# First attention: position tables in two sets of 64 rows, added in the tile shape of the paired scores, over their nonzero columns

## The reference, cut to what matters

```python
# DIM = 128, HEADS = 8, DIM_QK = 64, MAX_POS = 10; x is [4, 1024, 128]
x = x + attention(layernorm(x))
def attention(x):
    q, k, v = projections(x)                      # 8 heads of 64 (q, k) and 16 (v)
    dots = einsum('bhid,bhjd->bhij', q, k) * 64 ** -0.5
    dist = clip(seq[None, :] - seq[:, None], -10, 10) + 10
    attn = softmax(dots + conv[:, dist])          # conv is [8, 21]
    return (attn @ v) @ W_out + b_out
x = x + graph_of_six_attention_nodes(layernorm(x))
```

## Time and profile before

| | before |
|---|---|
| median of 3 runs | 3493.89 us (3486.42 to 3496.42) |
| the profiled execution's own time | 3510.56 us |
| its span | 3508.8 us |
| PE busy | 3152.7 us (90%), 18239 matmuls |
| DVE busy | 2418.2 us (69%) |
| ACT busy | 2154.6 us (61%) |
| mean granted TensorE clock | 0.922 of 2.4 GHz |

### The profile page before, as it was taken

How to read it: one execution, slowest core, us unless ns; L and a number is a source line. 1 busy time by engine, 2 the same in 40 slices (tenths; PEclk the granted TensorE clock), 3 DMA queues, 4 the chain that set the end, 5 groups by cost and what they waited for, 6 DMA issues and landing times. The chain is left out here.

```text
span 3508.8 us, 47634 instructions
## 1 busy us (share of the span) xinstructions
PE 3152.7 (90%) x18239; PEld 1353.8 (39%) x18239; DVE 2418.2 (69%) x3087; ACT 2154.6 (61%) x2695; POOL 389.8 (11%) x330
## 2 busy tenths in 40 slices
PE   5799999999748999999999999999999999999994
PEld 4355555555423333333333333333333333333331
DVE  5545544545146678888788788888778888787753
ACT  1144544544513467777777777777777777777683
POOL 0000000000010011111101111111111111111013
PEclk9699999999955589999999999999999999999897
DMA  5000000000043244344343344434444344443302
GB/s 160 16 10 4 22 1 10 16 10 10 17 119 73 46 94 100 89 96 91 77 95 90 79 100 102 100 90 96 75 92 94 91 94 85 102 100 86 60 22 80
DMA packets 144026, 244.99 MB, mean 70 GB/s; under 512 B 56290, under 2 KB 92534, under 8 KB 140726
## 3 DMA queue, kind: packets, MB, share of 16 engines
q1 hardware_dynamic: 143222, 239.85, 30.4%
q10 hardware_dynamic: 576, 2.10, 0.1%
HBM read 165.00 MB, written 74.10 MB: 68 GB/s over the span
## 5 line engine op out<-in xcount | busy, mean ns | idle before, releaser
L1395 ACT ACTIVATE pt_b<-ps_max 128x1024 f32<-128x1024 f32 x1516 | 1496.0, 1024 | 528.1 <-PE ps_max L1246 523.5
L1428 DVE TENSOR_REDUCE mx_b<-ps_pair 128x2 f32<-128x1024 f32 (+1 forms) x1032 | 1244.8, 1206 | 262.3 <-PE ps_pair L1232 255.4
L1282 PE MATMUL ps_ctx<-pt_b,vs 128*32 128x512 f32 x6144 | 866.6, 638 | 3.8 <-ACT c_b L1384 3.5
L1428 DVE TENSOR_REDUCE mx_b<-ps_misc 128x1 f32<-128x512 f32 x1032 | 706.2, 684 | 191.5 <-PE ps_misc L1232 174.7
L1246 PE MATMUL ps_max<-qs,ks 50*128 50x512 f32 x3032 | 828.6, 453 | 3.7 <-DMA qs<-mpart 3.1
L1232 PE MATMUL ps_pair<-ks,qs 48*128 48x512 f32 x2040 | 571.6, 487 | 128.2 <-DVE mx_b L1428 99.4
L1232 PE MATMUL ps_misc<-ks,qs 48*128 48x512 f32 x1032 | 491.8, 477 | 54.3 <-DVE mx_b L1428 47.8
L1246 PEld LDWEIGHTS ps_max<-qs,ks 50*128 50x128 f32 x3032 | 383.4, 196 | 354.5 <-ACT pt_b L1395 231.4
L1232 PEld LDWEIGHTS ps_pair<-ks,qs 48*128 48x128 f32 x2040 | 236.2, 197 | 462.2 <-DVE mx_b L1428 391.1
L740 ACT ACTIVATE pt<-ps_max,cb 128x512 f32<-128x512 f32 x342 | 215.6, 684 | 292.1 <-PE ps_max L617 227.6
L1232 PEld LDWEIGHTS ps_misc<-ks,qs 48*128 48x128 f32 x1032 | 204.5, 198 | 413.7 <-DVE mx_b L1428 332.7
(11 more groups left out here) (178 smaller groups left out, 2421.3 us busy)
## 6 DMA issues: line engine op xcount, KB each, us to landing
partd<-part SPq DMA_DIRECT2D x24, 2048.0 KB, 9.1
qs<-partd SPq DMA_DIRECT2D x288, 128.0 KB, 5.6
ks<-partd SPq DMA_DIRECT2D x288, 128.0 KB, 6.7
xq<-node SPq DMA_DIRECT2D x24, 512.0 KB, 3.9
xk<-node SPq DMA_DIRECT2D x24, 512.0 KB, 4.9
xv<-node SPq DMA_DIRECT2D x24, 512.0 KB, 5.8
xf<-node SPq DMA_DIRECT2D x24, 512.0 KB, 4.7
node<-nt_b SPq DMA_DIRECT2D x48, 256.0 KB, 2.2
```

What stands on the lines that cost most here:

```text
L1282: ins = pe.matmul(psO[SLOT * i:SLOT * i + SLOT, :], vs[u % 2][:, kb, QUAD * (s // HALF_STEPS) + i], pt[:, (QUAD * S + i) % ENTRIES], start ...
L1395: act.activation(pt[:, e:e + 2].rearrange("p k n -> p (k n)"), at[:], ACT.Exp, scale=SCALE_B).then_inc(exp_done, 1)
L1428: nc.vector.tensor_reduce(mx2[:, at:at + n], (psP, psX)[p % 2][:, 0:CHUNK * n].rearrange("p (h n) -> p h n", h=n), AX.X, ALU.max).then_inc ...
```

## The change

The table matrix is cut into two sets of 64 rows (keys 0 to 63 and 64 to 127 of the block: b = 0 and 1), kept per head in the partitions of that head: even heads of a pair in partitions 0 to 63, odd heads in 64 to 127. Each set enters as a pair of 64-row matmuls, one for each head, in the same tile shape as the pairs of L612 and L588. The weights are `eye`: for set b the identity of 64 in columns 64 b to 64 b + 63 of a 64 x 128 matrix, zero elsewhere. `side_half` cuts the columns by which a set is zero. The widths become 74 and 138 columns (r = 0 and 3), 202 and 266 (r = 1 and 2), and 10 for one set alone (r = 4 and -1). A score round with a table so has 8 table matmuls in four pairs (10 columns: 4 in two pairs) where it had 4; a maxima round 4 in two pairs (10 columns: 2 in one) where it had 2. Each half gains 96 matmuls and 96 weight loads.

The prelude loads the tables by 16 DMAs where it had 4, each 64 partitions by 4 heads, and turns them with `flip`, two exchange matrices of 64 on the diagonal, which DVE builds (one memset and two copies) before its first layernorm. At the start of the first attention DVE clears `eye` and fills it with four copies, where it made one copy of the identity.

```diff
+def side_half(kb, qc, b):
+    s, lo, hi, at = side(kb, qc)
+    if hi and s == 0 and b == 0:
+        hi = max(0, hi - DQK)
+    if hi and s == 1 and b == 1:
+        lo, at = lo + DQK, at + DQK
+    return s, lo, hi, at
...
-                    sp.dma_start(tabf[:, k], bass.AP(ext.tensor, k * HEADS * NE + first, [[1, P], [NE, HEADS], [1, WIN]])
-                                 ).then_inc(tab_in, D16)
+                    for odd in range(2):
+                        for b in range(2):
+                            src = bass.AP(ext.tensor, (k * HEADS + odd) * NE + first + DQK * (1 - b),
+                                          [[1, DQK], [2 * NE, HEADS // 2], [1, WIN]])
+                            sp.dma_start(tabf[DQK * odd:DQK * odd + DQK, k, b], src).then_inc(tab_in, D16)
...
+                dve.wait_ge(id_in, 2 * D16)
+                nc.vector.memset(flip[:], 0.0).then_inc(flipped, 1)
+                dve.wait_ge(flipped, 1)
+                for k in range(2):
+                    rows = slice(DQK * k, DQK * k + DQK)
+                    ins = nc.vector.tensor_copy(flip[rows, rows], exch[rows, DQK * (1 - k):DQK * (2 - k)])
+                ins.then_inc(flipped, 1)
...
+                def windows_of(kb, qc):
+                    found = [(b, *side_half(kb, qc, b)) for b in range(2)]
+                    return [w for w in found if w[3] > w[2]]
...
# maxima
-                    for odd in range(2 if hi else 0):
-                        ins = pe.matmul(to[:, CHUNK * odd + lo:CHUNK * odd + hi], idr[:],
-                                        tabM[:, s, QUAD * q + 2 * j + odd, at:at + hi - lo], start=False, stop=True)
+                    for half_, s, lo, hi, at in windows:
+                        for odd in range(2):
+                            rows = slice(DQK * odd, DQK * odd + DQK)
+                            ins = pe.matmul(to[:, CHUNK * odd + lo:CHUNK * odd + hi], eye[rows, half_],
+                                            tabM[rows, s, half_, 2 * q + j, at:at + hi - lo], start=False,
+                                            stop=half_ == windows[-1][0])
...
# score
-                    for odd in range(2 if hi else 0):
+                    for half_, side_, lo, hi, at in windows:
                         for k in range(2):
-                            ins = pe.matmul(to[:, CHUNK * odd + lo:CHUNK * odd + hi], idr[:],
-                                            tabS[:, k, side_, QUAD * q + 2 * j + odd, at:at + hi - lo], start=False,
-                                            stop=k == 1)
+                            for odd in range(2):
+                                rows = slice(DQK * odd, DQK * odd + DQK)
+                                ins = pe.matmul(to[:, CHUNK * odd + lo:CHUNK * odd + hi], eye[rows, half_],
+                                                tabS[rows, k, side_, half_, 2 * q + j, at:at + hi - lo], start=False,
+                                                stop=k == 1 and half_ == windows[-1][0])
...
-                nc.vector.tensor_copy(idr[:], sid[:])
+                nc.vector.memset(eye[:].bitcast(F32), 0.0).then_inc(eye_cleared, 1)
+                dve.wait_ge(eye_cleared, 1)
+                for b in range(2):
+                    for odd in range(2):
+                        rows, cols = slice(DQK * odd, DQK * odd + DQK), slice(DQK * b, DQK * b + DQK)
+                        nc.vector.tensor_copy(eye[rows, b, cols], sid[rows, rows])
```

More of the change, by code:

```diff
@@ L128, in program @@
         stored = ctx.enter_context(nc.semaphore("node_stored"))
-        with nc.sbuf_tensor("tab_scores", [P, 2, 2, HEADS, WIN], F32R) as tabS, \
-                nc.sbuf_tensor("tab_maxima", [P, 2, HEADS, WIN], F32R) as tabM:
+        with nc.sbuf_tensor("tab_scores", [P, 2, 2, 2, HEADS // 2, WIN], F32R) as tabS, \
+                nc.sbuf_tensor("tab_maxima", [P, 2, 2, HEADS // 2, WIN], F32R) as tabM:
             prelude(nc, psM, psS, psX, sid, exchange, x_rows, conv, conv_rev, ew, act_w, We, be, Wq, Wk, Wv, Wo, ident,
@@ L178, in prelude @@
         wfs = sb("wfs", [P, NODES, WF_COLS])
-        tabf = sb("tabf", [P, 4, HEADS, WIN])
+        tabf = sb("tabf", [P, 4, 2, HEADS // 2, WIN])
         exch = sb("exch", [P, P])
+        flip = sb("flip", [P, P])
         x_in = [sem(f"x_in{b}") for b in range(BATCH)]
@@ L194, in prelude, with table @@
             sem("wb_copied"), sem("wo_ready"))
-        def table(n):
-            return tabS[:, 0, n // HEADS, n % HEADS] if n < 2 * HEADS else tabM[:, n // HEADS - 2, n % HEADS]
+        flipped = sem("flipped")
+        def table(n, k=0):
+            t, b, pair = n // HEADS, n % HEADS // QUAD, n % QUAD
+            return tabS[:, k, t, b, pair] if t < 2 else tabM[:, t - 2, b, pair]
         with nc.Block() as block:
@@ L275, in _ @@
                     pe.matmul(psX[:, 36:37], wnin[:, c, 3], bcol[:, 0:1], start=True, stop=True).then_inc(wb_ready, 1)
-                pe.wait_ge(tab_in, 4 * D16)
+                pe.wait_ge(tab_in, 16 * D16)
+                pe.wait_ge(flipped, 2)
                 for n in range(4 * HEADS):
@@ L280, in _ @@
                         pe.wait_ge(tab_copied[n % 2], n // 2)
-                    pe.matmul(psS[n % 2][:, 0:WIN], exch[:], tabf[:, n // HEADS, n % HEADS], start=True,
+                    pe.matmul(psS[n % 2][:, 0:WIN], flip[:], tabf[:, n // HEADS, n % HEADS // QUAD, n % QUAD], start=True,
                               stop=True).then_inc(tab_ready, 1)
@@ L385, in _ @@
                             dve.wait_ge(tab_high[0], n // 2 + 1)
-                        nc.vector.tensor_tensor(tabS[:, 1, (n + k) // HEADS, (n + k) % HEADS], psS[k][:, 0:WIN],
+                        nc.vector.tensor_tensor(table(n + k, 1), psS[k][:, 0:WIN],
                                                 table(n + k).bitcast(F32), ALU.subtract).then_inc(tab_copied[k], 1)
@@ L403, in first_attention @@
         pt = sb("pt", [P, 2, QUAD, CHUNK])
-        idr = sb("idr", [P, P], F32R)
+        eye = sb("eye", [P, 2, P], F32R)
         minus = sb("minus", [P, P], F32R)
@@ L430, in first_attention @@
         w_in, cb_in = sem("a_w_in"), sem("a_cb_in")
-        consts, padded = sem("a_consts"), sem("a_padded")
+        consts, padded, eye_cleared = sem("a_consts"), sem("a_padded"), sem("a_eye_cleared")
         xn_in, xr_in = sem("a_xn_in"), sem("a_xr_in")
@@ L584, in maxima @@
                     slot_free("maxima", hh, p)
-                    s, lo, hi, at = side(qb, kc)
+                    windows = windows_of(qb, kc)
                     for odd in range(2):
@@ L588, in maxima @@
                         ins = pe.matmul(to[:, CHUNK * odd:CHUNK * odd + CHUNK], qh[q][rows, j, P * qb:P * qb + P],
-                                        kh[q][rows, j, CHUNK * kc:CHUNK * kc + CHUNK], start=True, stop=hi == 0)
-                    for odd in range(2 if hi else 0):
-                        ins = pe.matmul(to[:, CHUNK * odd + lo:CHUNK * odd + hi], idr[:],
-                                        tabM[:, s, QUAD * q + 2 * j + odd, at:at + hi - lo], start=False, stop=True)
+                                        kh[q][rows, j, CHUNK * kc:CHUNK * kc + CHUNK], start=True, stop=not windows)
+                    for half_, s, lo, hi, at in windows:
[4 more added lines that the diff above has]
+                                            stop=half_ == windows[-1][0])
                     ins.then_inc(mx_ready, 1)
@@ L606, in score @@
                     kb, qc = s % KB, s // KB
-                    side_, lo, hi, at = side(kb, qc)
+                    windows = windows_of(kb, qc)
                     keys, queries = slice(P * kb, P * kb + P), slice(CHUNK * qc, CHUNK * qc + CHUNK)
@@ L613, in score @@
                                             minus[rows] if a is None else a[q][rows, j, keys], b[q][rows, j, queries],
-                                            start=a is kh and b is qh, stop=a is None and hi == 0)
-                    for odd in range(2 if hi else 0):
+                                            start=a is kh and b is qh, stop=a is None and not windows)
+                    for half_, side_, lo, hi, at in windows:
                         for k in range(2):
-                            ins = pe.matmul(to[:, CHUNK * odd + lo:CHUNK * odd + hi], idr[:],
-                                            tabS[:, k, side_, QUAD * q + 2 * j + odd, at:at + hi - lo], start=False,
-                                            stop=k == 1)
+                            for odd in range(2):
[3 more added lines that the diff above has]
+                                                stop=k == 1 and half_ == windows[-1][0])
                     ins.then_inc(s_ready, 1)
```

## The result

The changed kernel takes 3401.73 us (median of 4 runs, 3387.01 to 3439.62) against 3495.15 for the kernel before (4 runs): ratio 0.9701, 95% interval 0.9608 to 0.9793. Run again in 6 runs beside 11 of the kernel before it came out at 0.9767 (0.9718 to 0.9817). The ratios are worked out from runs no more than 1.5% above the fastest of their kernel, so they are not exactly the quotients of the medians.

What follows compares the result with a forecast made beforehand. PE was taken to bound the middle halves. Saving 62 us in seven halves and 6 in the last, 68 in all, took the median from 3493.9 to 3426 us (profiled 3510.56 to 3442.6); range 3404 to 3460.

Steps and rivals of the forecast that it cites:

- the step from the profiled execution to the median: Whole program: the median of runs lies 16.7 us below the profiled execution, so 3442.6 profiled became a 3426 us forecast.
- kept 8.9 us a half: Seven halves beside maxima: 11.5 us of PE work saved each, 2.6 returning as waits; 62 us in seven.
- PE is the bound, DVE in the lone maxima: Middle half: PE busy 94.49 of 98.30 us; maxima ahead of the first half: DVE busy 36.71 of 37.00, nothing gained.
- A pair costs 0.11: Table matmuls: a short 64-row pair costs 0.11 us, 0.13 for 266 columns; a 138-column score table 0.44.
- Rival 3: Table pairs: their weight loads don't overlap, 0.22 us each; 3485 us. Chance 0.05, shared with supply that eats the gain.
- Entering, leaving and drain go: Tables before 64-row work: shape changes (0.10 in, 0.11 out) and the 0.10 us drain vanish; scores save 0.36 to 0.53.
- The last half keeps 6: Last half, without maxima: score tables save 6.3 us, of which 6 are kept, ACT being far from its limit.
- The graph is unchanged: Graph after the first attention: no change expected, named as a sign that the forecast is right.
- Rival 2: Halves: fewer waits or more gained at half clock, all 11.5 us kept; 86 us saved, 3408 us. Chance 0.08.
- Rival 1: Halves: waits take more or pairs cost 0.13 to 0.16; 5 us a half kept, 3455 us. Chance 0.18.
- Rival 4: Middle halves: PE's instruction supply binds, deciding at 69 ns each; at 72 ns 27 us longer, 3521 us. Chance 0.05.
- Rival 5: Borders between halves: more idle holds PE at half clock, costing 7 x 2.5 = 17 us; no chance given.

Runs made afterwards that it cites:

- doubles_late: Changed kernel with the second of two maxima rounds in steps 3, 6, 9 and 12 moved behind the second score: 3415.40 us, ratio 0.9741 to before.

## Why the prediction was right and its size wrong

The mechanism was right, place by place. Two steps of the sum failed. The forecast was 24 us too high. 21 of that came with the step from the profiled execution to the median, 16.7 us taken as the program's own where 38 were measured. And the term "kept 8.9 us a half" was too small: 10.1 were kept at 2.4 GHz, and the seven halves gave 74.7 us for 62, of which the profiled time shows only part, since its graph took 7.2 longer than that of before. By the steps as the prediction put them:

- **PE is the bound, DVE in the lone maxima.** Right: 34.97 of 35.00 us on DVE there, and the first turn moved by 2.1 us at most.
- **A pair costs 0.11.** Right: 0.45 and 0.22 where 0.44 and 0.22 were worked out. Rival 3 (0.22 a pair) is out.
- **Entering, leaving and drain go.** Right. Step 2 of the fifth half saved 1.19 (by the prices 1.21), step 4 1.68 (1.63), step 11 1.56 (1.43), step 13 1.50 (1.42), step 14 0.66 (0.63), and steps 6 and 7 nothing and 0.46, as worked out.
- **"Kept 8.9 us a half."** This term was too small. Steps 2 to 15 of the fifth half saved 10.1. Step 5 gave 0.43 instead of 0.16, step 11 0.13 more than forecast, and step 15 0.33 instead of nothing: the wait at the border was taken to swallow all of what the last scores save, but the turn also comes 0.13 sooner behind a 64-row table (0.70 instead of 0.83), where the prediction had a loss of 0.05. The wait in step 3, the largest, was right (2.99 for 3.06). So 1.4 of the 11.5 is given back, not 2.6, which is 8 us in seven halves. The other 4 or so of the 12.7 missing ones lie in steps 11 to 13 of the fourth and sixth half, where the stretch at 1.2 GHz behind the output stall became shorter.
- **The last half keeps 6.** Steps 2 to 15 saved 4.8. In the profile the last half with what follows it is only 1.4 shorter, and 3.4 in the repeat; 45 us of the last half ran at a clock of 0.93, where before it was 1.00.
- **"The graph is unchanged."** Right for its work, but its time is not fixed: it varies with how long PE is granted 1.2 GHz, in a range (2510.70 to 2545.50) half as wide as the whole effect.
- **From the profiled execution to the median by 16.7 us.** This is the step that put the forecast outside. For the profiled execution the forecast was 3442.6, and 3439.62 was measured. The 16.7 was a difference between one run of before and the median of three, not a property of the program (no run shows it to be one). The four runs after have clocks of 0.922 for the profiled one and 0.932 to 0.940 for the others, and their median is 38 below the profiled one. The repeat, with six runs, has 3428.29, 2 us from the forecast.

Rival 2 (all 11.5 kept, 86 us, 3408) came nearest of the rivals, and at equal clock the change is worth 80 ± 2, nearer to rival 2's 86 than to the forecast's 68. The graph's start moved by 78.2 us in one profile and by 74.4 in the other; what lies between these and 80 is not shown to be more than scatter. Rival 1 (only 5 kept) is out: the slot waits grew, but took far less. Rival 4 (instruction supply) is out: a middle half had one matmul or load for each 63 ns (89.59 us for 709 and 710), where the point of decision was 69 ns, and the dense 15 us had one for each 51 ns (296), with PE busy 14.32 of them. The rule that the Trainium skill gives on it (TensorE: Matmul & The Clock Gate, What happens when you issue a matmul, some 62 ns for each MATMUL with hardware decode off) can hold here only if loads are not counted. Whether hardware decode was off, no run shows. Rival 5 (the borders at half clock, 35 us more of it) is out: the granted clock was at 1.2 GHz for 82.6 us of the attention before and for 74.8 and 77.0 after, and behind the output stalls for 20.4 instead of 34.1.

The prediction had said that the slot waits of steps 3, 6, 9 and 12 would grow, by 0.64, 0.41, 0.41 and 0.64. By what doubles_late and the same edit on the kernel before save in the first half, they grew by 0.53, 0.43, 0.20 and 0.50: 1.7 instead of 2.1.

What was not in the prediction: the two table loads beside the square root cost PE time, about as much in the kernel before (0.56 in a wait) as in the changed one (0.52), and more once the order of the rounds is changed. The wait of 4.7 us ahead of the output was known and rightly put at no change; that the clock behind it would gain from the change was not. The slot waits, the output's wait and the root are together worth 45 us of the attention (737.0 to 692.3).

## What to carry to other kernels

The short matmuls here were priced by their weight loads and by the change of tile shape around them, not by their columns. Before removing columns, count the pairs that go with them. When a PE-bound loop with few buffers becomes faster, look where two rounds of the same kind follow each other and what else sits in the queue of the engine that frees the buffers: here a short function with another table on ACT took 2.1 us of PE in a step. And where a program's clock varies from run to run, fit time against granted clock over all runs before a median of four is believed, and look at the runs that lie off the line: one of 110 moved a difference by 13 us here. To see whether two parts of a change add, compare a stretch that ran at one clock in all kernels.

## What the runs showed of the hardware

- With paired 64-row matmuls the loads of both row halves run beside each other. At 2.4 GHz a pair costs 0.23 us with 512 columns and 0.11 in the tables of 10 and of 138; 0.11 is the distance of two pairs of loads.
- Two loads of a function table on ACT for one small square root take 2.56 of 2.77 us. How much of it PE feels depends on the order of its work: in step 7 a wait of 0.56 us in the kernel before, 0.52 in the changed one, and 2.08 with one maxima round moved.
- A stall of PE costs more than itself. Behind 4.7 us of idle (the wait in front of L673) the granted level stood at 1.2 GHz for 6.8 to 17.1 us, and removing three such stalls (14 us) took 18 to 20 us off, net of the 2.4, 2.4 and 4.0 us that steps 12 to 14 gave back.
- One program on one core took 3465.52 to 3553.37 us (2.5%), the time following the granted clock. Between the two profiles of the changed kernel the whole difference (31.3 us of span) lies in the graph (34.8).
